# TensorE's order within one step of the attention stage: the mask product and the two score passes are placed differently

## The reference

```
x = x + tanh(g_xattn[0]) * long_convolution_mixer(ctx, ctx, layernorm(x))
x = x + tanh(g_ffn[0])   * (shared_gated_ffn + top2_of_8_experts)(layernorm(x))
x = x + tanh(g_xattn[1]) * causal_attention(layernorm(x), ctx, ctx)      # the change is here
x = x + tanh(g_ffn[1])   * (shared_ffn + top6_of_32_experts)(layernorm(x))
```

## Time and profile before

| | |
|---|---|
| median of 3 runs | 882.43 us (882.14 to 882.95) |
| the profiled execution's own time | 882.0 us |
| its span (first to last instruction) | 880.2 us |
| attention steps, first turns to the turns of quad 63 | 371.3 to 484.0 us |
| TensorE busy over the span | 98% |

### The profile page before, as it was taken

How to read it: one execution, slowest core, us unless ns; L and a number is a source line. 1 busy time by engine, 2 the same in 40 slices (tenths; PEclk the granted TensorE clock), 3 DMA queues, 4 the chain that set the end, 5 groups by cost and what they waited for, 6 DMA issues and landing times.

```text
span 880.2 us, 13926 instructions
## 1 busy us (share of the span) xinstructions
PE 859.6 (98%) x4764; PEld 710.5 (81%) x4764; DVE 589.6 (67%) x1226; ACT 533.2 (61%) x914; POOL 141.7 (16%) x125
## 2 busy tenths in 40 slices
PE   7999999999999999999999899999999999999997
PEld 6999887888788888877777678887788888888886
DVE  4998754565745655599998766659655465666664
ACT  3334443444643444567796767777777877777774
POOL 6996100010112110023232500000000000000000
PEclk9999999999999999999999999999999999999999
DMA  8230232436323431033433054444444344444433
GB/s 281 112 120 31 87 100 99 126 108 194 103 98 116 144 127 65 21 99 110 130 113 99 20 174 141 130 125 143 144 144 126 120 140 146 146 144 144 143 120 108
DMA packets 68390, 106.47 MB, mean 121 GB/s; under 512 B 9121, under 2 KB 31937, under 8 KB 67937
## 3 DMA queue, kind: packets, MB, share of 16 engines
q1 hardware_dynamic: 68112, 105.49, 38.0%
q10 hardware_dynamic: 208, 0.09, 0.0%
HBM read 96.81 MB, written 8.74 MB: 120 GB/s over the span
## 4 chain that ended last, share of the span: by engine, by line
PE 82%; DVE 9%; DMA 2%; issue 2%; POOL 2%; ACT 1%; SPq 1%; DVEq 0%; ACTq 0%; POOLq 0%
PE bank L700 37%; PE bank L736 29%; PE bank L1581 3%; PE bank L1592 2%; PE bank L1215 1%; PE bank L1216 1%; PE bank L1482 1%; PE bank L1572 1%; DVE max L1772 1%; DVE y L1778 1%; PE bank L1566 1%; PE bank L1234 1%; PE bank L384 1%; DMA x_mixed<-in_x 1%; PE bank L1601 1%
## 5 line engine op out<-in xcount | busy, mean ns | idle before, releaser
L497 ACT ACTIVATE y_hi<-y 128x512 fp32r<-128x512 f32 x200 | 124.2, 622 | 81.2 <-DVE y L580 80.4
L594 DVE TENSOR_TENSOR y<-y,gate_rows 128x512 f32<-128x512 f32 x124 | 85.8, 692 | 116.7 <-ACT y L486 115.0
L736 PE MATMUL bank<-y_hi,w_hi 128*128 128x512 f32 x400 | 157.0, 392 | 2.1 <-DVE y_lo L331 1.5
L736 PE MATMUL bank<-y_hi,w_lo 128*128 128x512 f32 x400 | 155.8, 390 | 0.0
L736 PE MATMUL bank<-y_lo,w_hi 128*128 128x512 f32 x400 | 155.7, 389 | 0.0
L331 DVE TENSOR_TENSOR y_lo<-y,y_hi 128x512 fp32r<-128x512 f32 x196 | 134.4, 687 | 30.0 <-ACT y_hi L497 29.6
L480 ACT ACTIVATE activated<-bank 128x512 f32<-128x512 f32 x136 | 81.2, 597 | 77.3 <-PE bank L700 70.1
L700 PE MATMUL bank<-x_hi_first,w_hi 128*128 128x512 f32 x264 | 105.1, 398 | 0.7 <-DVE w_lo L326 0.7
L700 PE MATMUL bank<-x_hi_last,w_hi 128*128 128x512 f32 x264 | 104.0, 394 | 0.0
L700 PE MATMUL bank<-x_hi_first,w_lo 128*128 128x512 f32 x264 | 103.0, 390 | 0.0
L700 PE MATMUL bank<-x_hi_last,w_lo 128*128 128x512 f32 x264 | 102.9, 390 | 0.0
(11 more groups left out here) (157 smaller groups left out, 1358.1 us busy)
## 6 DMA issues: line engine op xcount, KB each, us to landing
gate_rows<-gates SPq DMA_DIRECT2D x156, 256.0 KB, 3.7
w_raw<-in_wu SPq DMA_DIRECT2D x68, 256.0 KB, 2.6
w_raw<-in_wu SPq DMA_DIRECT2D x32, 384.0 KB, 4.1
k_blocks<-k_parts SPq DMA_DIRECT2D x128, 64.0 KB, 2.2
k_parts<-xn_split SPq DMA_DIRECT2D x32, 128.0 KB
v_slot<-in_v_rows SPq DMA_DIRECT2D x16, 256.0 KB, 3.0
ctx_windows<-in_ctx_win SPq DMA_DIRECT2D x3, 1024.0 KB, 13.8
x_mixed<-in_x SPq DMA_DIRECT2D x4, 512.0 KB, 9.5
```

What stands on the lines that cost most here:

```text
L497: act.activation(mem.yhi[:, K % S, :], mem.y[:, K % S, :], ACT.Copy).then_inc(s_yh, 1)
L594: dve.tensor_tensor(mem.y[:, K % S, :], mem.y[:, K % S, :], gate, ALU.mult).then_inc(s_yd, 1)
L736: last = pe.matmul(acc(s)[:, c, :], w_[:, Nu % S, wc], y_[:, K % S, :], start=(n == 0 and m == 0), stop=(n == U - 1 and m == 2), skip_grou ...
```

## The change

A step of TensorE becomes: turns of quad n, mask of quad n+3, second score pass of quad n+2, values of quad n-1, first score pass of quad n+3; then what belongs to the place t, as before. So the mask and the first pass of a quad are made one step earlier than before, and the second pass of the next quad stands right behind a mask. Before the loop, mask and first pass of quad 2 are made. The first pass waits for its keys and, at t = 0, for the first half of the turned queries (s_qt >= 2b+1); the second pass waits at t = 0 for the other half (2b+2). Quads 0 and 1, whose scores are made in f0's last products, keep the old order. No product is added or left out.

```diff
-            def scores(pe, n):
-                b, t = n // 4, n % 4
+            def masked(pe, n):
                 if n == 0:
                     pe.wait_ge(s_cc, 32)
                 if n >= SR:
                     pe.wait_ge(s_d, n - SR + 1)
                 pe.matmul(s_bank(n), identb[:], causal[:].rearrange("p h k -> p (h k)"), start=True, stop=False)
+
+            def pair_scores(pe, n, a):
+                b, t = n // 4, n % 4
+                blocks = K1[:, n % KR, :].rearrange("p (h a k) -> p h a k", h=2, a=2)
+                return pe.matmul(s_bank(n)[:, a * 2 * P:(a + 1) * 2 * P], Q1[:, b % 2, a, t, :], blocks[:, :, a, :],
+                                 start=False, stop=(a == 1))
+
+            def first_scores(pe, n):
+                b, t = n // 4, n % 4
                 pe.wait_ge(s_kl[n % KR], LOADED + 32 * (n // KR + 1))
                 if t == 0:
+                    pe.wait_ge(s_qt, 2 * b + 1)
+                pair_scores(pe, n, 0)
+
+            def last_scores(pe, n):
+                b, t = n // 4, n % 4
+                if t == 0:
                     pe.wait_ge(s_qt, 2 * b + 2)
-                blocks = K1[:, n % KR, :].rearrange("p (h a k) -> p h a k", h=2, a=2)
-                for a in range(2):
-                    last = pe.matmul(s_bank(n)[:, a * 2 * P:(a + 1) * 2 * P], Q1[:, b % 2, a, t, :], blocks[:, :, a, :],
-                                     start=False, stop=(a == 1))
-                last.then_inc(s_s, 1)
+                pair_scores(pe, n, 1).then_inc(s_s, 1)
+
+            def scores(pe, n):
+                masked(pe, n)
+                first_scores(pe, n)
+                last_scores(pe, n)
...
             def c_tensor(pe):
                 pe.wait_ge(f0.s_os, 3)
+                masked(pe, 2)
+                first_scores(pe, 2)
                 for n in range(NQ):
                     b, t = n // 4, n % 4
                     turned(pe, n)
                     if n == 0:
                         pe.wait_ge(s_qt, 4)
                         f0.out_turned(pe, 1, 0, 0, x_bank)
+                    if n + 3 < NQ:
+                        masked(pe, n + 3)
                     if n + 2 < NQ:
-                        scores(pe, n + 2)
+                        last_scores(pe, n + 2)
                     if n == 0:
                         pe.wait_ge(f0.s_os, 4)
                         f0.out_turned(pe, 1, 0, 1, row_bank)
                     if n > 0:
                         values(pe, n - 1)
+                    if n + 3 < NQ:
+                        first_scores(pe, n + 3)
```

## The result

| | before | changed |
|---|---|---|
| median (17 runs each) | 882.43 us (881.18 to 887.24) | 885.69 us (883.98 to 889.26) |
| the profiled execution's own time | 882.0 | 885.19 |
| its span | 880.2 | 883.4 |

The ratio is 1.0037, with a 95% interval of 1.0024 to 1.0051: slower. The median lies 3.26 us above the one before and 0.1 us above the end of the forecast range. They are in the medians, the ranges and the ratios.

The account below looks back on a forecast made before the run. TensorE was taken to bound mid-attention, VectorE the start up to turns 14. Start 0.34, steps 1.82, end -0.33 and 0.02 summed to +1.85 us: median from 882.43 to 884.3 us, range 882.9 to 885.6.

Parts of the forecast that it names:

- The price of the passage out of the values: Behind the values, a score pass's load exposes 0.11 us instead of a transpose's 0.057: +0.052 or +0.03 a step.
- The 0.12 of a pass in either place: The moved score pass takes 0.12 us away before the values and adds 0.12 back behind them.
- The start: Quad 2's mask and first pass ahead of turns 0 delay line 259, then VectorE up to turns 14: +0.34 us.
- The end: Quad 64 does not exist, so step 61 loses mask and first pass: -0.33 us; turns 62 give +0.02 back.
- The covered steps: Steps 43, 44, 45 and 51, where chains over VectorE cover what is added to TensorE.
- The sum of the stage: The attention's terms together: 0.34 + 1.82 - 0.33 + 0.02 = +1.85 us.
- the 43 steps that count: Steps 14 to 42, 46 to 50, 52 to 60, bound by TensorE: 24 x 0.052 + 19 x 0.03 = +1.82 us.
- The failed step: Whole kernel: the attention's +1.85 us carried over to the profiled execution (883.9) and the median (884.3 us).
- Nothing elsewhere: Keys, the mask's wait for the shift and the query copies, all wanted earlier, were claimed to add no delay.
- The exposed load vanishes: Rival: the score pass's load is pulled ahead of the values' end, 879.6 us; chance 0.07, shared with another case.
- The load costs its whole 0.19: Rival: the pass's load behind the values exposes 0.19 us instead of 0.11, 3.4 more, 887.7 us; chance 0.08.
- More is covered: Rival: VectorE bounds more steps than counted, or f0's output is no brake at the start: +1.0, 883.4 us; chance 0.15.

Follow-up runs that it names:

- e3_pass_ahead: Changed kernel, but the first pass of quad n+3 stands in front of the values, behind the second pass of n+2: median 883.88 us, ratio 1.0006.
- e4_late_start: Changed kernel, but quad 2's mask and first pass are made in step 0 instead of ahead of turns 0: median 884.28 us, ratio 1.0015.
- e10: The kernel before, unedited, run again to see how its times spread: median 882.94 us, ratio 1.0008.
- e1_again: The changed kernel, unedited, run again: median 887.68 us, ratio 1.0048.
- e11: The changed kernel, unedited, run a third time: median 885.09 us, ratio 1.0030.
- e14: Second run of the changed kernel with the DMA of x's second block issued earlier: median 883.37 us, ratio 1.0011.
- e2_mask_last: Against the kernel before, only the mask of quad n+3 goes behind the values, both passes staying together in front: median 880.72 us, ratio 0.9982.
- e8_filler: The kernel before plus one bf16 product of 32 columns behind the values of every step: median 883.56 us, ratio 1.0018.
- e6_after_early_x: The changed kernel with the DMA of x's second block issued earlier: median 884.78 us, ratio 1.0022.

## Why the prediction was right or wrong

**The price of the passage out of the values: right.** The pass behind the values takes 0.39 (0.388 in the row of one), as forecast (0.278 and 0.11; 385 to 388 ns for twelve of them from 420 to 440 us); no turns in the middle steps take 330 ns (270 to 295 from 420 to 440); a batch went from 6.69 to 6.84 where 6.70 to 6.86 was forecast. e3_pass_ahead, which takes only that load away, has 6.69 again. That shows the cause. The load behind the values starts 0.07 us ahead of the recorded end of the last of the values' products, in the kernel before (430.99 and 431.06) as in the changed one (433.09 and 433.16); what it waits for up to that point no run shows. The gap and the price are as read.

**The 0.12 of a pass in either place: right.** The sum has it as 0.12 away and 0.12 back, and no row shows it for the new places: it was the author's estimate from the 0.24 for two. In the changed kernel one pass less between mask and values took 0.11 off (0.54 to 0.43), and behind the values it is 0.23 from the pass's start to the first turn (433.09 to 433.32), 0.12 beside the exposed 0.11. The loads of the two passes in the kernel before, 0.19 each, start 0.03 and 0.11 us ahead of their products (430.09 and 430.12, 430.31 and 430.42), while the product in front is still running (430.09 to 430.47 and 430.12 to 430.59).

**The start: right.** Turns 14 came 0.33 later (forecast 0.34), and e4_late_start gave 0.26 of it back. Line 259 starts 1.66 us after f0's last product and started 1.30 after it (372.46 less 371.16): 0.36 more. The time on the clock, forecast as 372.8, was 374.01, because f0 itself had ended 1.2 us later.

**The end: right.** Step 61 became 0.31 shorter (forecast 0.33), and turns 62 wait 0.03 longer for VectorE (forecast 0.02).

**The covered steps: right.** The chain around steps 43 to 46 goes over the reciprocal, shifts, maxima and line 340, as in the earlier trace rows, and turns 46 wait for the shift still; what was added there is absorbed. So is it in step 51.

**The sum of the stage** was +1.85 and is +1.72 (112.86 to 114.58): the 43 steps that count gave 1.69 where 1.82 was forecast. The profiled execution's rest, 0.3 us, and the time ahead of the attention, 1.2 us, came on top.

**The failed step** is the one behind the sum: "The profiled execution would go from 882.0 to 883.9, the median from 882.43 to 884.3 us". It went to 885.19, the median to 885.69. I carried the stage's delay over to the whole as if all else stood still (under "Nothing elsewhere" only keys, mask and queries are asked about), and made the range (882.9 to 885.6) out of the bounds of the load's price alone. The first stage does not stand still: x landed 1.1 us later in the profiled execution, and the profiled executions with a stall of 2.3 us or so there (2.34 in e10, 2.4 in e3), followed by a granted clock of 0.50, are some 5 us longer (in the four profiled ones f0's last product starts 2.6 to 5.5 us later than in the kernel before). One set's median of the same kernel, e1_again, lay 2.0 us above the other, and e11 0.6 below it. The term of the attention was right; with the spread outside it, the range should have reached one to two us further up. In the profiled executions what goes beyond the 1.7 us lies outside the attention, at the landing of x and at two DMAs of gate rows (VectorE's waits at 219 and at 514 us), and it did not repeat in e1_again and e14. For the median of 17 it is not shown where the remaining 1.5 us lie: over the five pairs of sets the medians differ by 1.35 to 5.1 us and the fastest executions by 1.7 to 2.8. Whether all of that was chance, or the new order also draws more long executions, stays open.

**The rivals.** *The exposed load vanishes*: no. The gap of 0.20 stands on the pass's load at 60 places. The load of the transposes behind the pass is another matter: it starts 0.10 ahead of their first product (433.22 and 433.32) and under the pass (433.09 to 433.48). *The load costs its whole 0.19*: no, the product is 0.39 and not 0.47. *More is covered*: no; VectorE's fewer waits (9 with 3.5 us for 12 with 6.0) took up only what had been counted. A gain was within reach, but by another edit: the same passage with the mask first.

## What to carry to other kernels

Behind a group of narrow products after which the next weight load starts late (0.20 us behind the last one here), put a product that has to be made anyway, has many columns (512 here; 256 hid the next load too, 32 did not) and a weight load that exposes little: here the bf16 mask, which exposes 0.01 us, where an fp32 transpose exposes 0.057 and an fp32r pass 0.11; between e2_mask_last and the changed kernel that choice was 0.35 us a batch and, with the start, 4.0 us in all. Only this one group, eight products of 32 output columns, was tested. Read such a price from the duration of the first product behind the group less that of its fellows elsewhere, not from the length of the load's own row. And when a stage's delay is carried over to the median, look first at how far the rest of the program moves between executions: here one stage was forecast to 0.13 us while the median of the same kernel moved by 2 between sets.

## What the runs showed of the hardware that was not expected

- A product of 32 columns behind the values, whose own load starts with it (both at 431.52 in e8_filler), did not shelter the load that follows: four transposes behind it took 0.64 us against 0.66 right behind the values and 0.60 behind a pass of 256 columns, and the stage grew by 0.94 us.
- Where TensorE had been busy only 1.6 to 1.7 of 4 us, the granted clock fell to 0.50, in four profiled executions at two places (e3_pass_ahead at 25 us; e6_after_early_x, e10_before_null and e11_after_third at 77 to 81 us); a pair of the convolution's products then took 0.60 us where it took 0.30 at a granted clock of 1.00, by the chain of e3_pass_ahead:

```profile
24.49 0.30 PE bank L1215 x2
...
25.67 0.60 PE bank L1216 x2
26.27 0.60 PE bank L1215 x2
```

  That is no rule that can be forecast from: from 8 to 12 us the kernel before was busy 0.97 of 4 us and its granted clock stayed at 1.00, while e10_before_null, the same kernel, was busy 0.70 there and its clock fell to 0.50 at 12.6 us.

- The same DMA of x, with nothing in front of it edited, landed 1.1 us apart in two executions (18.76 and 19.87; half of that was there when it was issued, at 10.94 and 11.46), and VectorE's first moments, and what follows them, moved with it.
- VectorE's one wait for the gate rows near 514 us took from 1.42 to 2.48 us over the profiled executions and moved the whole second feed-forward with it, in both orders.
